# Cross-attention kernel: contiguous score tiles of 128 successive queries, log-sum rows copied in runs of 32, scores ahead of the output product in step 1, text value weight split one block later

## The reference, cut to what matters

```python
q = _heads(hidden_states @ to_q_w)                 # 20 heads of 32 channels
h_txt = _sdpa(q, _heads(ehs_txt @ to_k_w), _heads(ehs_txt @ to_v_w))
h_obj = _sdpa(q, ...object weights...); h_oth = ...; h_ip = ...
out = _merge(h_txt) + _merge(h_obj) + _merge(h_oth) + _merge(h_ip)
out = out @ to_out_w + to_out_b + residual
```

## Time and profile before

| | us |
|---|---|
| median of 3 runs | 2648.68 (2648.46 to 2649.89) |
| the profiled execution | 2657.83 |
| its span, first to last instruction | 2655.9 |
| PE busy over the span | 2537.1 (96%) |
| ACT busy | 1723.4 (65%) |
| DVE busy | 1623.1 (61%) |
| POOL busy | 407.8 (15%) |
| part one ends at about | 945 |

### The profile page before, as it was taken

The page is one execution under the profiler, slowest core; times in us unless marked ns, Lnnn a source line. Parts: engine busy times, 40 slices in busy tenths (PEclk is TensorE's granted clock), DMA queues, the critical chain, the costliest instruction groups (busy, mean ns, idle before and its releaser), DMA issues.

```text
span 2655.9 us, 37372 instructions
## 1 busy us (share of the span) xinstructions
PE 2537.1 (96%) x13125; PEld 1931.1 (73%) x13125; DVE 1623.1 (61%) x2964; ACT 1723.4 (65%) x3830; POOL 407.8 (15%) x564
## 2 busy tenths in 40 slices
PE   7999999999999947999999999999999999999997
PEld 7999999999999934566666666666666666666664
DVE  3131111111111048888888888888888888888882
ACT  3131222121212127999999999999999999999993
POOL 0000000000000022122122122122221221221210
PEclk9999999999999968999999999999999999999999
DMA  8473333232323156566666666566566666666642
GB/s 227 123 238 121 120 112 124 101 125 101 125 101 125 74 125 122 97 138 139 126 141 133 128 136 142 120 146 139 116 145 139 122 138 138 129 136 130 136 98 65
DMA packets 256898, 341.25 MB, mean 128 GB/s; under 512 B 48446, under 2 KB 150974, under 8 KB 256710
## 3 DMA queue, kind: packets, MB, share of 16 engines
q1 hardware_dynamic: 203312, 275.93, 45.5%
q10 hardware_dynamic: 53398, 62.93, 6.9%
HBM read 186.71 MB, written 83.89 MB: 102 GB/s over the span
## 4 chain that ended last, share of the span: by engine, by line
PE 41%; DVE 14%; issue 5%; ACT 4%; DMA 1%; SPq 0%; DVEq 0%
PE m_ps L869 10%; PE s_ps L797 8%; PE o_ps L825 8%; PE m_ps L846 7%; PE st_ps L811 7%; DVE negmax L980 4%; DVE q_out L1031 2%; DVE small L987 2%; DVE q_out L1028 2%; ACT probs L916 2%; DVE heads L1041 2%; ACT s_ps L924 2%; DVE heads L1046 1%; DVE neglse L1013 1%; DVE neglse L1011 0%
## 5 line engine op out<-in xcount | busy, mean ns | idle before, releaser
L924 ACT ACTIVATE s_ps<-s_ps,negmax 128x427 f32<-128x427 f32 x1280 | 760.5, 599 | 73.0 <-DVE small L987 72.9
L980 DVE TENSOR_REDUCE negmax<-s_ps 128x2 f32<-128x854 f32 x640 | 663.1, 1036 | 149.6 <-PE s_ps L797 147.9
L916 ACT ACTIVATE probs<-st_ps 128x1024 f32<-128x1024 f32 x640 | 661.6, 1034 | 91.0 <-PE st_ps L811 91.0
L797 PEld LDWEIGHTS s_ps<-kpack,qpack 96*128 96x128 f32 x1280 | 348.1, 312 | 205.7 <-issue 114.6
L797 PE MATMUL s_ps<-kpack,qpack 96*128 96x512 f32 x1280 | 450.6, 434 | 37.6 <-ACT s_ps L924 31.0
L464 PE MATMUL v_ps<-w_split,ctx_split 128*128 128x320 f32 (+2 forms) x3072 | 453.6, 309 | 0.0
L464 PEld LDWEIGHTS v_ps<-w_split,ctx_split 128*128 128x128 f32 (+2 forms) x3072 | 451.5, 186 | 0.7 <-issue 0.5
L447 PE MATMUL k_ps<-ctx_split,w_split 128*128 128x428 f32 (+2 forms) x2280 | 429.0, 349 | 11.1 <-DVE k_out L391 6.5
L447 PEld LDWEIGHTS k_ps<-ctx_split,w_split 128*128 128x128 f32 x2280 | 411.0, 190 | 26.6 <-DVE k_out L391 6.8
L811 PE MATMUL st_ps<-qpack,kpack 104*128 104x512 f32 x1280 | 409.4, 401 | 8.7 <-ACT probs L916 6.1
L391 DVE TENSOR_TENSOR k_out<-k_ps,k_out 128x427 fp32r<-128x427 f32 (+2 forms) x97 | 56.1, 578 | 545.7 <-ACT k_out L287 545.7
(11 more groups left out here) (54 smaller groups left out, 1466.4 us busy)
## 6 DMA issues: line engine op xcount, KB each, us to landing
kpack<-kT SPq DMA_DIRECT2D x240, 256.0 KB, 5.4
qpack<-q_out SPq DMA_DIRECT2D x240, 256.0 KB, 5.6
kT<-k_out ACTq DMA_DIRECT2D x160, 217.5 KB, 2.2
ctx_split_raw<-in_ctxT SPq DMA_DIRECT2D x128, 214.0 KB, 4.4
xs_raw<-in_xT SPq DMA_DIRECT2D x80, 256.0 KB, 5.8
out<-in_xT SPq DMA_DIRECT2D x80, 256.0 KB, 6.1
out_yT<-out SPq DMA_DIRECT2D x80, 256.0 KB, 3.3
v_ip_rows<-v_out ACTq DMA_DIRECT2D x48, 320.0 KB
```

What stands on the lines that cost most here:

```text
L797: last = nc.tensor.matmul(s_ps[:, n % 2, z, :], queries_of(r, j, t), kpack[0:ROWS_S, r, j, :], start=True, stop=True)
L916: nc.scalar.activation(probs[:, at:at + 2, :], st_ps[:, :, :], ACT.Exp).then_inc(p_done, 1)
L924: last = nc.scalar.activation(s_ps[:, n % 2, z, SMALL:TOK], s_ps[:, n % 2, z, SMALL:TOK], ACT.Exp, bias=negmax[:, r, IP, j, t:t + 1], accu ...
L980: nc.vector.tensor_reduce(negmax[:, r, IP, j, t0:t0 + 2], s_ps[:, n % 2, :, SMALL:TOK], AX_X, ALU.max, negate=True).then_inc(s_max, 1)
```

## The change

There are four edits. The stationary operand of `scores` becomes 128 successive queries, `qpack[.., t * P:(t + 1) * P]`, a contiguous read. To match, the transpose writes `lse_t` in the order (t i) instead of (i t), and each of the 4 DMAs of `pack_lse` writes runs of 32 elements instead of 128. In step 1 (`S_EARLY`) of every slot, PE issues `scores` ahead of the product. And in part one the eight pieces of the text value weight are split at blocks ("k", 1, 1) to ("k", 1, 4) instead of ("k", 1, 0) to ("k", 1, 3).

```diff
-        spread("w", "v_txt", ("k", 1, 0), (2, 2, 2, 2))
+        spread("w", "v_txt", ("k", 1, 1), (2, 2, 2, 2))
...
 Y_LAG = 9
+S_EARLY = 1
...
-        def queries_of(r, j, t):
-
-            return qpack[0:ROWS_S, r, j, :].rearrange("c (i t) -> c t i", t=QT)[:, t, :]
-
...
                 for b in range(QT):
-                    sp.dma_start(qpack[ROWS_S:ROWS_ST, u % QKR, :, b * P:(b + 1) * P].bitcast(F32),
-                                 lse_t[b * TURN:(b + 1) * TURN, :].bitcast(F32)).then_inc(lse_packed[u % QKR], 16)
+                    rows = qpack[ROWS_S:ROWS_ST, u % QKR, :, :].bitcast(F32).rearrange("c j (t b i) -> c j t b i", t=QT, b=QT)
+                    sp.dma_start(rows[:, :, :, b, :], lse_t[b * TURN:(b + 1) * TURN, :].bitcast(F32)
+                                 .rearrange("c (t i) -> c t i", t=QT)).then_inc(lse_packed[u % QKR], 16)
...
-                    last = nc.tensor.matmul(s_ps[:, n % 2, z, :], queries_of(r, j, t),
+                    last = nc.tensor.matmul(s_ps[:, n % 2, z, :], qpack[0:ROWS_S, r, j, t * P:(t + 1) * P],
                                             kpack[0:ROWS_S, r, j, :], start=True, stop=True)
...
-                    products_at(m, k)
+                    if k != S_EARLY:
+                        products_at(m, k)
                     u, p = pair_at(m, k + 1) if k + 1 < STEPS else pair_at(m + 1, 0)
                     if unit(u):
                         scores(u, p)
+                    if k == S_EARLY:
+                        products_at(m, k)
...
-                nc.vector.transpose(lse_t[:, :].bitcast(F32).rearrange("c (i t) -> c t i", t=QT), ...)
+                nc.vector.transpose(lse_t[:, :].bitcast(F32).rearrange("c (t i) -> c t i", t=QT), ...)
```

More of the change, by code:

```diff
@@ L1020, in turn_lse @@
                     dve.wait_ge(lse_packed[(u - 1) % QKR], 16 * QT * use(u - 1, QKR))
-                nc.vector.transpose(lse_t[:, :].bitcast(F32).rearrange("c (i t) -> c t i", t=QT), neglse2[:, :, :, :, :].bitcast(F32).rearrange("p t a g j -> p t (a g j)")).then_inc(lse_turned, 1)
+                nc.vector.transpose(lse_t[:, :].bitcast(F32).rearrange("c (t i) -> c t i", t=QT), neglse2[:, :, :, :, :].bitcast(F32).rearrange("p t a g j -> p t (a g j)")).then_inc(lse_turned, 1)
             def keep_queries(u):
```

## The result

The changed kernel takes 2660.6 us (median of 20 runs, 2652.82 to 2664.34), the kernel before 2652.46 on the same chips (20 runs, 2648.46 to 2658.28). The ratio is 1.0027, with a 95% interval of 1.002 to 1.0034: slower by a little, 7.2 us on the median of before (0.0027 x 2652.46), where the prediction had 6.5. In absolute terms it had 2655, which is 5.6 short: it started from the median of 3 runs of before, 2648.68, and the 20 runs have 3.8 more. The profiled execution took 2661.36 us with a span of 2659.5, 3.6 more than before's 2655.9. The 20 executions of the changed kernel lie up to 11.5 us apart, so the intervals weigh more than a difference of two spans.

What follows compares the result with a forecast made beforehand. PE was taken to bound the slot, with one gap waiting for DVE. 57 x 0.09 + 14 x 0.1 = 6.5 us on 2648.68 gave 2655 us, range 2649 to 2661, 8 in 10 2643 to 2668.

Steps and rivals of the forecast that it cites:

- A wait for ACT takes the place of the wait for DVE: Step 1: scores moved ahead wait for ACT's exponentials; PE restarts 6.18 us after step 6's scores, not 5.91, +0.27 a slot.
- The gap of 0.4 us: PE's idle time each slot ahead of the first output matmul, waiting for DVE's `q_out`; forecast not to be filled.
- Contiguous loads: Weight load of `scores` falls from 312 to 190 ns; step 4 and six hidden pairs save about 0.18 us a slot.
- step 0: Its shorter load of `scores` behind the values lies inside the 5.70 us with PE's wait, changing only that wait; nothing.
- The sum: Ordinary slot +0.27 - 0.18 = +0.09 us; 57 such slots and 14 at 0.1 make 6.5 us.
- The slots in which POOL splits `x`: 14 of 71 slots, where DVE's `neglse` waits for POOL: between 0 and +0.25 us each, taken as 0.1.
- Log-sum rows: Four DMAs with 512 runs of 128 bytes: at most 2.2 us later, covered by 2.9 before step 6; price 0.
- Transpose and weight split: Transpose on DVE ahead of step 3's `negmax`: 0; text value weight splits end 0.5 us before use: taken 0.
- did the pair go without a wait: Rival: step 1's scores don't wait for ACT, the gap is filled; -40 us, 2608; 0.12 together with a smaller gain.
- the loads stay long: Rival: weight loads of `scores` don't get faster, +0.27 us in 71 slots at most, +19 us, 2668; chance 0.05.
- a log-sum row come late: Rival: step 6 waits from 2.9 us later on; at 0.3 us over the cover 2676; chance 0.03.
- The clock: Rival: PE's longer gap drops its clock to 1.2 GHz in single slots; five such slots make 2662; chance 0.08.

Runs made afterwards that it cites:

- Experiment 2: The kernel before with only the scores of step 1 moved ahead of the output product, strided loads kept; 2677.91 us, 1.009 of before.
- experiment 1: The changed kernel with scores back behind the output product in step 1, so the layout edits and later weight split alone; 2645.89 us, 0.9967 of before.
- experiment 4: The changed kernel with ACT's second exponentials of `small` moved from step 7 to step 0 of the next slot; 2643.0 us, 0.9956 of before.
- experiment 5: Contiguous tiles, output product ahead of scores in step 1, ACT's second exponentials of `small` moved to the next slot's step 0; 0.9976 of before.
- Experiment 6: Contiguous tiles, output product ahead of scores in step 1, one query matmul moved from step 6 to step 7; 2631.34 us, 0.9921 of before.
- experiment 3: The kernel before with only the later split of the text value weight; 0.9998 of before.
- experiment 8: The changed kernel, ACT's second exponentials of `small` moved to the next slot, one query matmul from step 6 to 7; 2634.33 us, 0.9926 of before.

## Why the prediction was right

**A wait for ACT takes the place of the wait for DVE.** Right, and its size too: restart at 6.16 us for 6.18. Experiment 2 shows the longer stretch with the order alone and experiment 1 its absence without the order. Experiments 4 and 5 show that ACT's block is the cause, and only in the new order. What made this forecast possible was the earlier trace rows: the new order already stood in the trace of before, in slots that had no output product yet. The gap of 0.4 us that the order might have filled was not there to be had, since ACT releases the pair later than DVE releases the output. Experiment 6 fills it with a matmul that waits for neither.

**Contiguous loads.** Right: 192 ns for 190, and 0.66 behind the values for 0.67. A fell by 0.17 us (0.18 in experiment 1) where the sum had 0.18. The rule of the Trainium skill on the page "TensorE: Matmul & The Clock Gate", section "LDWEIGHTS (loading the stationary operand)", by which only the number of columns counts, would have made this nothing. The trace doesn't agree, with 312 ns against 192 for one and the same load under two layouts. What the prediction left out is that the strided load would cost more in the new order (0.87 for 0.73 at the restart). It had rightly counted step 0 as nothing in the old one, and the changed kernel has the short load everywhere, so the sum didn't suffer.

**The sum.** +0.27 - 0.18 = +0.09 us in ordinary slots; measured +0.08 by the medians of 42 of them, and +0.23 and -0.17 for the two parts by the chain. The 14 ordinary slots behind a slot with POOL's split got longer by some 0.23. The prediction had no term for that.

**The slots in which POOL splits `x`.** The term was +0.1 us each, with bounds of 0 and 0.25. In the two profiled executions these slots were 0.19 us shorter on average, outside the bounds. The profile of experiment 3 is a second execution of before's code in part two, and in it they are 0.15 shorter than in before's: most of the difference is scatter. Against experiment 3 the slots with the split are 0.04 us shorter after, and the ones behind them 0.22 longer. As pairs they are 0.18 longer (0.10 against before, without the pair in which the clock fell), and the prediction's two terms for such a pair make 0.19. So the size is borne out for a pair, roughly. It lies in the slot behind and not in the one that the prediction named, and why was not tried.

A look at one of these slots misleads. The operation of DVE on `neglse` that takes 1.39 us in the earlier trace rows takes 0.29 in the same slot of the changed kernel, but there the cast just ahead of it takes 1.34 in place of 0.52. In each of the 14 slots, before and after, at least one of the operations on `neglse` takes 1.3 to 1.4 us; which one differs from slot to slot in either kernel.

That the total came so close (7.2 for 6.5, with an interval from 5.3 to 9.0) is luck in part. The 56 ordinary intervals add up to 5.1 us in the profiles, as the sum's 57 x 0.09 do, but out of other parts: 3.2 from 42 slots and 3.0 from 13, less 1.1 for the one that the clock had made long in before. The range of 2649 to 2661 given for this case is also wider than its own terms, which make 2650 to 2659.

**Log-sum rows.** Priced at 0, right. Two steps of the working don't hold. The number of dimensions doesn't stay: the destination of each DMA has one more. The issue of the four takes 2.96 us in place of 2.89, so this cost little. And doubled times for each run would not have been covered by the prediction's own bound: 5.0 us later against 2.9 of cover. The packets were short instead. The last of the 512 packets of 128 bytes had moved by 1519.6, and the weight load of step 6 comes at 1522.45; before, the last of the 128 packets had moved by 1520.4 and the load came at 1523.37. The cover is 2.9 us in both.

**Transpose and weight split.** Both priced at 0. The transpose got 93 ns shorter, but DVE isn't waited for there. The split ends 0.40 us ahead of its use (forecast 0.5), and experiment 3 has it at 0.9998.

**The rivals.** Neither did the pair go without a wait, nor the loads stay long, nor a log-sum row come late. The clock was 1.00 from 1135 to 2555 in the profiled execution of the changed kernel. The one fall in that part was in before's, at 1459.6. So falls in single slots, of which the prediction speaks, do occur, and the profile of experiment 8 has one too, at 1454.7. Whether the new order makes them more frequent, one profile of each kernel can't show.

## What to carry to other kernels

Moving work ahead of a wait fills the wait only if the moved work isn't released later than the waiting one. Here PE restarts 0.25 us later on the moved pair than it did on the result that the old order waited for. Once ACT's block was shorter, the same order gained 0.07. Look for a stretch elsewhere in the trace (the start or the end of a pipeline) in which the new order already runs; it gives the price without a model. And where another engine sets the length of a stretch and PE waits at its end, move PE's work into it: moving one matmul in a table gave 0.46% here (0.9967 to 0.9921), more than the whole change took (0.27%). The room is limited: in experiment 8 the same matmul brought PE's own work onto the chain.

## What the runs showed of the hardware

- The stationary operand read with a step of 4 elements (16 bytes) loads in 312 ns, contiguous in 192, with the same 96 x 128 elements.
- The 32 x 32 block transpose of 128 x 128 elements on DVE writes contiguous rows in 312 ns, rows with a step of 16 bytes in 405.
- From SBUF to SBUF a packet of 128 bytes takes 13 ns by the packet records, one of 512 bytes 27 (median): four times the packets took about twice the time. The Trainium skill ("DMA: Bandwidth & Descriptors", section "Specifications") has a read-modify-write under 512 bytes; if there is one, it doesn't lift the small packet's time to that of the larger one here.
- A matmul of 128 x 512 moved into a stretch that DVE sets cost 0.02 us in place of 0.23 (experiment 6); where the stretch had been made shorter first, it cost 0.09 (experiment 8 against 4).
